# Attention with a spline feed-forward layer: chunk 2 staged ahead of the first feed-forward tile, and three moves ahead of it

## The chip, the cores and the metric

One of the cores of a Trainium2 chip runs the whole kernel. The metric is the device time of one execution in microseconds (us), as the median of several. The engines are named as in the profile: PE (TensorE, matmuls and transposes), PEld (its weight loads), DVE (VectorE), ACT (ScalarE), POOL (GpSimd) and SP (SyncE, which here only issues DMAs; ACT has a DMA queue of its own, ACTq).

## The reference

x has shape (4, 512, 512). Cut to what matters:

```python
xn = layernorm(x)                                  # last axis
q, k, v = xn @ Wq + bq, xn @ Wk + bk, xn @ Wv + bv # 16 heads of 32
scores = q k^T / sqrt(32) + slope(head) * distance(key), causal
attn = softmax(scores) v ;  a = attn @ Wo + bo
gate_w, up_w = spline(gate_cp), spline(up_cp)      # (2048, 512), Catmull-Rom
down_w = spline(down_cp)                           # (512, 2048)
f = (silu(xn @ gate_w.T) * (xn @ up_w.T)) @ down_w.T
out = x + a + f
```

The dense weights of the feed-forward layer are interpolated from about 8,100 control points each: every weight is a blend of four neighbouring points with cubic coefficients.

## The kernel before

The kernel has two parts that every engine runs one after the other: `attention` for all four batches, then `ffn`. Both keep fp32 accuracy by splitting operands into a rounded high part and a remainder ("hi" and "lo") and multiplying in three terms. Each engine's order is written out by hand; semaphores connect the engines, and an engine that waits holds up all that stands behind it in its list. SP issues its DMAs in list order too.

Attention. A batch has H = 16 steps, one per head, and each step has four query tiles. In step s, PE makes the scores of head s (line 689), DVE adds the distance bias and takes the maximum (`bias_and_max`, line 910), ACT takes the exponentials and casts them (lines 1143, 1151), POOL makes their low part (line 1256), PE turns the probabilities of step s-2 (line 703) and weighs the values of step s-3 (lines 720, 723). DVE and ACT copy the turned tiles (lines 919, 1158), DVE normalizes (928 to 936). `UNITS`, `TURNS` and `SPLITS` say in which step a projection, a transposition or a split of the values stands; the next batch's layer norm and projections are carried along in steps 7 to 15 of the running batch. Scores take queries and keys from stacks that SP copies there after POOL's low part (line 1311). `v_split` (lines 889 to 900) makes three bf16 parts of the values of one token tile in three DVE instructions, behind a first cast on ACT (`v_high`, line 1136). In the first batch the values of tiles 0 to 3 are taken ahead of step 0, tiles 0 and 1 are split at the end of step 0 together with tile 2, and tile 3 in step 1 (`FIRST_SPLITS`).

Layer norm of a later batch: DVE makes mean and variance (`pair_stats`), POOL the inverse deviation (line 1244), DVE the shift -mean * rstd (`norm_shift`, line 869), and ACT applies both in one activation per tile (line 1103) in steps 8 and 9.

Weights of the feed-forward layer. They come in five chunks: chunk 0 for down, chunks 1 to 4 for gate and up, four tiles of 128 rows in each. A chunk is a load of blend factors (1 MB) and one of control windows ("taps", 1 MB), seven DVE instructions that blend them (`taps_op`, lines 343 and 348, 0 to 6), a split into high (ACT, `taps_high`, line 358) and low (DVE, `taps_low`, line 368) for the two halves m = 0, 1 of the partitions, and DMAs that copy each half across to the other 64 partitions (`copy_across`, lines 376 and 380, four of 128 KB for chunks 1 to 4). The input of gate and up is the tile z: windows of the turned input (line 330) and moments of it over pieces (line 335), loaded per tile and per quarter of four tiles. Moments are products of bases with the turned input; the last batch's are made in the attention part, the others in `ffn` (kind "mom").

`ffn` runs the batches in the order 3, 0, 1, 2, with 16 tiles of the hidden dimension each. `ffn_order` writes PE's order: for each tile k "gu" (four matmuls, lines 1588 and 1589), in the first batch a "gen" (four matmuls, lines 1576 and 1577) that makes one tile of the down weights, and "down" of tile k-2 (twelve matmuls, lines 1601 to 1603). A generated tile goes through ACT (`down_start`, 1642), DVE (`merge`, 1706), ACT (`down_high`, 1656) and DVE (`down_low`, 1710). Two gens stand ahead of tile 0; `GEN_FRONT` and `GEN_BACK` place the others. `TAPS` places the blending of chunks 2 (its low split only), 3 and 4 on DVE, `HIGHS` their high split on ACT, and ACT issues the copies a tile later. In the first batch gate and up always use the same pair of banks.

At the seam SP's list is: the moments of the last batch, bases for gen, windows of tiles 0 to 3, moments, bases, the turned input of the next batch (two loads of 1 MB), factor 3, windows of tiles 4 to 7, moments, three attention sums (line 1328), taps 3 and 4, the fourth sum; then, once all sums are stored (line 1824), factor 4, bases, windows of tiles 8 to 15 and moments. DVE's list there: the last low context (943), the output sums (950) with the blending of chunk 2 and the low split of chunk 1 between them.

## Time and profile before

| | |
|---|---|
| median of 3 runs | 746.64 us (746.29 to 746.75) |
| the profiled execution | 748.68 us, span 746.9 us, mean granted clock 0.975 |
| PE busy | 673.0 us (90%) |
| PEld, DVE, ACT, POOL busy | 540.0, 463.3, 451.8, 322.3 us |
| DMA traffic | 110.15 MB, mean 147 GB/s |
| chain that ended last | PE 42%, POOL 5%, DVE 4%, issue 4%, ACT 2%, DMA 2% of the span |

Sizes of the transfers at the seam, from the page's list of DMA issues: factor and taps 1024 KB each, a load of turned input 1024 KB, bases for gen 512 KB, a window load 88 KB (two per tile), a moment load 160 KB, a copy across 128 KB, an attention sum 256 KB.

Busy shares are means over the whole span; matmuls overlap, and a busy PE is not one at its peak. The granted clock is the share of 2.4 GHz that PE was allowed in a stretch. A row of a timeline has its start and length in us; what stands in brackets at its end is the time for which the engine had been idle and what released it ("issue": nothing that the profile shows as an engine's work, often a DMA).

### The profile page before, as it was taken

The page shows a single profiled execution, that of the slowest core. Times are in us where ns is not written, and L with a number is a line of the kernel's source. Part 1 is how long each engine was busy: PE and PEld are TensorE (multiplying, and loading weights), DVE is VectorE, ACT ScalarE, POOL GpSimd, SP SyncE. Part 2 cuts the span into 40 slices and gives each one's busy share as a digit, 9 for nine tenths or more (in the row PEclk, how much of TensorE's full clock was granted, in tenths as well). Part 3 has the DMA queues.
Part 4 walks back from the last instruction along what each step waited for, and adds up shares of the span by engine and source line. Part 5 has one row for each costly group of instructions (what it writes and reads, how often), then busy time and mean ns, then how long its engine had stood idle before and what let it go on. Part 6 is the DMA issues. An engine that isn't in the chain of part 4 may idle for free.

```text
span 746.9 us, 13707 instructions
## 1 busy us (share of the span) xinstructions
PE 673.0 (90%) x4884; PEld 540.0 (72%) x4884; DVE 463.3 (62%) x1287; ACT 451.8 (60%) x717; POOL 322.3 (43%) x188
## 2 busy tenths in 40 slices
PE   4977889989799898899898876888999999999997
PEld 3756678777577776777776665666888888888885
DVE  6477977879877879778799796567441223223212
ACT  5478887877977878878779763444442332332221
POOL 0255554544644545545546430222253236236334
PEclk9988999999999999999999999899999999999999
DMA  9749497476676384863947939874576484244001
GB/s 304 115 71 225 86 259 128 64 135 169 94 204 86 43 140 98 216 86 57 208 76 97 400 97 271 255 220 113 163 245 213 130 244 166 70 143 140 13 1 56
DMA packets 53355, 110.15 MB, mean 147 GB/s; under 512 B 6504, under 2 KB 6760, under 8 KB 51752
## 3 DMA queue, kind: packets, MB, share of 16 engines
q1 hardware_dynamic: 51704, 106.85, 58.6%
q10 hardware_dynamic: 1584, 2.43, 1.3%
q8 instruction: 39, 0.64, 0.4%
q14 instruction: 28, 0.23, 0.1%
HBM read 59.32 MB, written 25.17 MB: 113 GB/s over the span
## 4 chain that ended last, share of the span: by engine, by line
PE 42%; POOL 5%; DVE 4%; issue 4%; ACT 2%; DMA 2%; ACTq 0%; SPq 0%; POOLq 0%; DVEq 0%
PE bank L1601 6%; PE bank L1603 6%; PE bank L1602 6%; PE bank L1588 3%; PE bank L1589 3%; POOL resid L1769 3%; PE bank L615 3%; PE bank L703 3%; PE bank L617 2%; PE bank L616 2%; DMA taps<-windows 2%; PE bank L689 2%; POOL in_lo L1761 1%; PE bank L1576 1%; PE bank L720 1%
## 5 line engine op out<-in xcount | busy, mean ns | idle before, releaser
L1256 POOL TENSOR_TENSOR work<-work 128x1280 f16<-128x1280 f32 x64 | 170.9, 2670 | 174.2 <-ACT work L1151 174.2
L1761 POOL TENSOR_TENSOR in_lo<-inner,in_hi 128x512 fp32r<-128x512 f32 x64 | 83.0, 1299 | 200.0 <-ACT in_hi L1668 200.0
L910 DVE CUSTOM_DVE_ANT_0 work<-bank,dist 128x128 f32<-128x128 f32 (+3 forms) x256 | 115.3, 487 | 59.4 <-PE bank L689 44.9
L1143 ACT ACTIVATE work<-work,neg_max 128x128 f32<-128x128 f32 (+3 forms) x256 | 129.3, 562 | 18.2 <-DVE neg_max L910 18.1
L1718 DVE TENSOR_TENSOR inner<-bank,silu 128x512 f32<-128x512 f32 x64 | 44.1, 688 | 132.3 <-ACT silu L1662 130.7
L1668 ACT CAST in_hi<-inner 128x512 fp32r<-128x512 f32 x64 | 39.7, 620 | 135.2 <-PE bank L1603 134.4
L703 PE MATMUL bank<-ident,work 128*128 128x128 f16 x1280 | 106.0, 226 | 14.6 <-DVE work L919 10.3
L703 PEld LDWEIGHTS bank<-ident,work 128*128 128x128 f16 x1280 | 75.4, 101 | 51.3 <-issue 31.8
L1151 ACT CAST work<-work 128x1280 f16<-128x1280 f32 x64 | 80.6, 1259 | 49.8 <-PE bank L703 48.6
L1601 PE MATMUL bank<-w_room,in_hi 128*128 128x512 f32 x256 | 100.0, 391 | 0.7 <-POOL in_lo L1761 0.7
L1602 PE MATMUL bank<-w_room,in_hi 128*128 128x512 f32 x256 | 99.6, 389 | 0.0
L1603 PE MATMUL bank<-w_room,in_lo 128*128 128x512 f32 x256 | 99.6, 389 | 0.0
L689 PE MATMUL bank<-k_stack,q_stack 96*128 96x256 f32 (+2 forms) x256 | 76.2, 373 | 22.4 <-DVE neg_max L910 18.3
L919 DVE COPY work<-bank 128x256 f16<-128x256 f16 (+2 forms) x192 | 75.6, 418 | 5.8 <-PE bank L703 5.7
L689 PEld LDWEIGHTS bank<-k_stack,q_stack 96*128 96x128 f32 x256 | 45.5, 195 | 38.7 <-DVE neg_max L910 29.6
L720 PE MATMUL bank<-v_parts,work 128*128 128x98 bf16 x640 | 66.7, 211 | 2.0 <-issue 2.0
L1158 ACT COPY work<-bank 128x1024 f16<-128x1024 f16 x64 | 64.4, 1006 | 2.5 <-PE bank L703 2.5
L723 PE MATMUL bank<-v_parts,work 128*128 128x66 bf16 x640 | 64.1, 195 | 0.0
L1588 PE MATMUL bank<-z,wgu_hi 128*128 128x512 f32 x128 | 52.2, 408 | 11.6 <-issue 7.5
L1601 PEld LDWEIGHTS bank<-w_room,in_hi 128*128 128x128 f32 x256 | 48.4, 189 | 12.0 <-POOL in_lo L1761 2.0
L720 PEld LDWEIGHTS bank<-v_parts,work 128*128 128x128 f16 x640 | 52.7, 99 | 5.6 <-issue 2.8
L1602 PEld LDWEIGHTS bank<-w_room,in_hi 128*128 128x128 f32 x256 | 48.1, 188 | 9.9
(113 smaller groups left out, 1313.9 us busy)
## 6 DMA issues: line engine op xcount, KB each, us to landing
q_stack<-parts SPq DMA_DIRECT2D x48, 256.0 KB, 5.8
k_stack<-parts SPq DMA_DIRECT2D x48, 256.0 KB, 6.2
z<-xt_scratch SPq DMA_DIRECT2D x128, 88.0 KB
x_in<-x SPq DMA_DIRECT2D x32, 256.0 KB, 6.7
xt_scratch<-xt_room SPq DMA_DIRECT2D x8, 1024.0 KB, 7.5
xt_room<-xt_scratch SPq DMA_DIRECT2D x6, 1024.0 KB, 10.6
factor<-c_basis SPq DMA_DIRECT2D x5, 1024.0 KB, 11.8
taps<-windows SPq DMA_DIRECT2D x5, 1024.0 KB, 15.8
```

The costliest lines, as they stand in the source:

```text
L689: pe.matmul(score_bank[i % 2][:, 0:n], q_stack[:, at, h, i * P:(i + 1) * P], k_stack[:, at, h, 0:n], start=True, stop=True).then_inc(s_ful ...
L703: mm = pe.transpose(pt_bank[i % 2][:, (part * n + k) * P:(part * n + k + 1) * P], probs16[:, s % 2, part, OFF[i] + k * P:OFF[i] + (k + 1) ...
L720: pe.matmul(bank[:, i * VALUES:(i + 1) * VALUES], probs_t[:, s % 2, at:at + P], v_parts[:, k, s, :], start=(k == 0), stop=False)
L910: dve.tensor_tensor_reduce(probs[:, s % 2, OFF[i]:OFF[i] + n], score_bank[i % 2][:, 0:n], dist[:, S - n:S], -slope(s), 3.4e38, ALU.add, AL ...
L919: dve.tensor_copy(probs_t[:, s % 2, 2 * OFF[i]:2 * OFF[i] + n], pt_bank[i % 2][:, 0:n]).then_inc(pt_free[i % 2], 1)
L1143: e = act.activation(tile, tile, ACT.Exp, bias=neg_max[:, s % 2, i:i + 1], scale=-1.0)
L1151: act.copy(probs16[:, s % 2, 0, :], probs[:, s % 2, :]).then_inc(hi_ready, 1)
L1256: pool.tensor_tensor(probs16[:, s % 2, 1, :], probs[:, s % 2, :], probs16[:, s % 2, 0, :], ALU.subtract).then_inc(lo_ready, 1)
L1601: pe.matmul(sum_bank[i][:, :], hi, wd_hi[:, g, :], start=(g == 0), stop=False)
L1602: pe.matmul(sum_bank[i][:, :], hi, wd_lo[:, g, :], start=False, stop=False)
L1603: mm = pe.matmul(sum_bank[i][:, :], lo, wd_hi[:, g, :], start=False, stop=(g == NG - 1))
L1761: pool.tensor_tensor(in_lo[k % 2][:, :], inner[:, k % 2, :], in_hi[:, k % 2, :].bitcast(F32), ALU.subtract).then_inc(il_ready, 1)
```

## The change

- The value splits of tiles 0 to 2 of the first batch stand between the takings of the values, ahead of step 0, and that of tile 3 in step 0. ACT's four first casts all stand ahead of step 0.
- For later batches DVE makes only -mean (with the statistics), and ACT multiplies it with the inverse deviation, one [128 x 1] activation per tile, ahead of its norm_apply.
- The first blending instruction of chunk 1 moves from step 12 to step 13 of the last batch.
- `taps_low` and `copy_across` wait for their own half m only. Of chunk 1's high casts on ACT one moves behind the last context cast; on DVE its low splits stand around `ctx_low`.
- All copies across of chunks 1 to 4 are issued by SP, no longer by ACT: chunk 1's behind the first moments, chunk 2's behind the moments of quarter 1, chunk 3's behind the windows of tiles 8 to 15, chunk 4's between the moment stores.
- SP loads the turned input of the next batch right after the moments' stores; taps 3 stands among the windows of tiles 4 to 7, taps 4 behind all four sums.
- Only one gen stands ahead of tile 0, the others one tile later; gen 10 stands behind tile 10's gate and up. Chunk 2 is split high and low around gen 0's first steps, ahead of tile 0.

```diff
+        def taps_high(act, c, some=(0, 1)):
-            eng.wait_ge(made_hi[c], 2)
+            eng.wait_ge(made_hi[c], m + 1)          # taps_low
-            eng.wait_ge(made_lo[c], 2)
+                eng.wait_ge(made_lo[c], m + 1)      # copy_across, per m
...
-FIRST_SPLITS = {0: [(0, 2)], 1: [(0, 3)]}
+FIRST_SPLITS = {0: [(0, 3)]}
...
+            if later(b):
+                dve.tensor_scalar(minus_mean[:, two], meanvar[:, two, 0], -1.0, None, ALU.mult).then_inc(mean_ready, 1)
...
-            if carry and s in (8, 9):
-                norm_shift(b + 1, s - 8)
-            if not later(b) and s == 0:
-                v_split(b, 0, 0)
-                v_split(b, 0, 1)
...
             v_take(0, t)
+            if t < 3:
+                v_split(0, 0, t)
...
-            if s >= H - 4:
+            if s == H - 3:
+                taps_op(dve, 1, 0)
+            if s >= H - 3:
                 taps_op(dve, 1, s - H + 4)
...
+        taps_low(dve, 1, 0)
         ctx_low(B - 1, KC - 1)
+        taps_low(dve, 1, 1)
...
+        def norm_shift(b, n):                       # on ACT
+            act.wait_ge(mean_ready, 2 * (b - 1) + n + 1)
+            act.wait_ge(rstd_ready, 2 * b + n + 1)
+            for t in (2 * n, 2 * n + 1):
+                act.activation(shift[:, t:t + 1], minus_mean[:, t:t + 1], ACT.Copy, scale=rstd[:, t:t + 1]
+                               ).then_inc(shift_ready, 1)
...
-        for t in range(3):
+        for t in range(QT):
             v_high(0, 0, t)
...
-                taps_high(act, 1)
+                taps_high(act, 1, (0,))
         ctx_high(B - 1, KC - 1)
+        taps_high(act, 1, (1,))
         act.activation(warm[:], ident[0:1, 0:1], ACT.Silu)
-        copy_across(act, 1)
...
+        sp.wait_ge(xt_st, 32 * B)
+        load_turned(sp, 1)
         sp.wait_ge(lo_ready, H * B)
...
         load_moments(sp, 0, 0)
+        copy_across(sp, 1)
         load_pieces(sp, 1)
-        load_turned(sp, 1)
         load_factor(sp, 3)
         sp.wait_ge(av_full, H * B)
-        for g in range(4, 8):
+        for g in range(4, 6):
+            load_windows(sp, 0, g)
+        sp.wait_ge(pj_full, pj_total(("o", QT - 1), B - 1))
+        load_taps(sp, 3)
+        for g in range(6, 8):
             load_windows(sp, 0, g)
         load_moments(sp, 0, 1)
-        for q in range(QT - 1):
+        copy_across(sp, 2)
+        for q in range(QT):
             store_sum(B - 1, q)
-        sp.wait_ge(pj_full, pj_total(("o", QT - 1), B - 1))
-        load_taps(sp, 3)
         load_taps(sp, 4)
-        store_sum(B - 1, QT - 1)
...
-GEN_FRONT = {k: k + 2 for k in range(MOM_STEPS[0] + 1)}
-GEN_BACK = {k: k + 1 for k in range(MOM_STEPS[1] + 1, NG - 1)}
+GEN_FRONT = {k: k + 1 for k in range(MOM_STEPS[0] + 1)} | {MOM_STEPS[1] + 1: MOM_STEPS[1] + 1}
+GEN_BACK = {-1: 0} | {k: k + 1 for k in range(MOM_STEPS[1] + 1, NG - 1)}
-    order = [("gen", 0, 0, 1), ("gen", 1, 0, 1)]
+    order = [("gen", GEN_BACK[-1], 0, 1)]
-TAPS = {1: [(2, 7)], 2: [(3, 0), (3, 1)], 3: [(3, 2), (3, 3)], 4: [(3, 4), (3, 5), (3, 6)], 5: [(3, 7), (4, 0)],
-        6: [(4, 1), (4, 2)], 7: [(4, 3), (4, 4)], 8: [(4, 5), (4, 6)], 9: [(4, 7)]}
-HIGHS = {0: 2, 4: 3, 8: 4}
+TAPS = {2: [(3, 0), (3, 1)], 3: [(3, 2), (3, 3), (3, 4)], 4: [(3, 5), (3, 6)],
+        5: [(3, 7), (3, 8), (4, 0)], 6: [(4, 1), (4, 2)], 7: [(4, 3), (4, 4)], 8: [(4, 5), (4, 6)], 9: [(4, 7), (4, 8)]}
+HIGHS = {4: 3, 8: 4}
...
-        for g in range(2):                          # ffn_scalar
-            down_start(g)
-            down_high(g)
+        taps_high(act, 2, (0,))
+        down_start(0)
+        taps_high(act, 2, (1,))
-                if n - 1 in HIGHS:
-                    copy_across(act, HIGHS[n - 1])
...
-        for g in range(2):                          # ffn_vector
-            merge(g)
-            down_low(g)
+        taps_low(dve, 2, 0)
+        merge(0)
+        taps_low(dve, 2, 1)
...
-        for g in range(8, 12):                      # ffn_sync
-            load_windows(0, g)
-        load_moments(0, 2)
+        for q in (2, 3):
+            for g in range(4 * q, 4 * q + 4):
+                load_windows(0, g)
+            load_moments(0, q)
+        copy_across(sp, 3)
         sp.dma_start(bm[:].bitcast(F32).rearrange("p k e n -> p (k e n)"), moment_d).then_inc(bm_ld, 16)
-        for g in range(12, NG):
-            load_windows(0, g)
-        load_moments(0, 3)
         load_pieces(3)
-        for m in range(3):
-            store_moment(1, m)
+        store_moment(1, 0)
+        store_moment(1, 1)
+        copy_across(sp, 4)
+        store_moment(1, 2)
```

## Rows read from the trace of the kernel before

**Rows 1.** Windows: stretch, length, busy (xcount) of PE PEld DVE ACT POOL, clock
```profile
100.00:140.00 40.00, 39.77 (x360) 31.80 (x361) 29.14 (x98) 31.50 (x48) 19.67 (x9) 1.00 0.78 184
```

**Rows 2.** Timeline, prologue: start, length, engine, line, operation, [idle before <-releaser]
```profile
38.55 2.88 DVE L896 TENSOR_TENSOR v_room<-v_room,v_parts 128x256 f32<-128x256 f32 x1
...
43.28 0.29 DVE L910 CUSTOM_DVE_ANT_0 work<-bank,dist 128x128 f32<-128x128 f32 x1
...
60.30 0.29 DVE L910 CUSTOM_DVE_ANT_0 work<-bank,dist 128x128 f32<-128x128 f32 x1 [3.77 <-issue]
...
24.36 4.76 POOL L1277 TENSOR_TENSOR w_room<-work,w_room 128x1024 fp32r<-128x1024 f32 x2 [14.79 <-ACT w_room L1199]
...
38.51 2.63 POOL L1256 TENSOR_TENSOR work<-work 128x1280 f16<-128x1280 f32 x1 [9.39 <-ACT work L1151]
...
38.83 0.47 PE L689 MATMUL bank<-k_stack,q_stack 96*128 96x256 f32 x2 [2.15 <-issue]
```

**Rows 3.** The shift's line; the timeline of ACT; the groups of ACT
```profile
L869 DVE SCALAR_TENSOR_TENSOR shift<-meanvar,rstd x6: 554/956/1353, 85.3 to 297.9; 128x2 f32<-128x2 f32 x6
...
93.57 1.52 ACT L1103 ACTIVATE x_in<-x_in,shift,rstd 128x512 f32<-128x512 f32 x2 [0.55 <-DVE shift L869]
...
L1143 ACT ACTIVATE work<-work,neg_max 128x128 f32<-128x128 f32 x64 | 26.2, 410 | 8.1 <-DVE neg_max L910 8.1
...
L1237 ACT ACTIVATE warm<-ident 1x1 f32<-1x1 f32 x1 | 0.2, 202 | 0.0
```

**Rows 4.** Timeline of DVE and of PE, last batch, step 12
```profile
419.65 1.37 DVE L343 TENSOR_TENSOR taps<-taps,factor 128x512 f32<-128x512 f32 x1 [2.44 <-DMA taps<-windows]
...
417.94 0.40 PE L689 MATMUL bank<-k_stack,q_stack 96*128 96x256 f32 x2
```

**Rows 5.** Timeline of DVE, then of PE, where they waited
```profile
450.17 0.69 DVE L943 TENSOR_TENSOR ctx_t<-bank,ctx_t 128x512 fp32r<-128x512 f32 x1 [1.99 <-ACT ctx_t L1164]
...
464.33 0.77 PE L1588 MATMUL bank<-z,wgu_hi 128*128 128x512 f32 x1 [2.33 <-issue]
...
487.16 0.76 PE L1588 MATMUL bank<-z,wgu_hi 128*128 128x512 f32 x1 [2.95 <-issue]
...
504.40 0.50 PE L1588 MATMUL bank<-z,wgu_hi 128*128 128x512 f32 x1 [1.77 <-DVE inner L1718]
...
511.50 0.47 PE L1588 MATMUL bank<-z,wgu_hi 128*128 128x512 f32 x1 [2.27 <-issue]
```

**Rows 6.** The windows view of PE alone, before and after tile 8
```profile
464.33:511.50 47.17, 37.90 (x137) 0.87 0.82 239
...
511.50:549.00 37.50, 37.50 (x164) 1.00 0.48 139
```

**Rows 7.** Timeline of the DMA issues, on SP's and ACT's queue
```profile
450.85 0.82 SPq L335 DMA_DIRECT2D z<-moment_scratch  x2
...
452.11 0.97 SPq L314 DMA_DIRECT2D xt_room<-xt_scratch  x2
...
461.40 4.60 SPq L1328 DMA_DIRECT2D mid_scratch<-x_in  x3
...
466.06 1.10 SPq L305 DMA_DIRECT2D taps<-windows  x2
...
487.34 0.33 SPq L1825 DMA_DIRECT2D factor<-c_basis  x1
...
503.58 0.94 SPq L335 DMA_DIRECT2D z<-moment_scratch  x2
...
455.76 0.78 ACTq L380 DMA_DIRECT2D wgu_lo<-wgu_lo  x1
```

**Rows 8.** Landing of the copies, then the DMA view's issues
```profile
DMA to landing us min/median/max: 4.7/7.0/7.9
...
mid_scratch<-x_in SPq DMA_DIRECT2D x4, 256.0 KB, 15.3
```

**Rows 9.** Windows of SP: stretch, length, granted clock, DMA share, GB/s
```profile
444.00:448.00 4.00, 1.00 0.33 94
```

More of the change, by code:

```diff
@@ L351, in tiles_of @@
             return room[m * ZR:(m + 1) * ZR, m, 4 * (c - 1):4 * c, :].rearrange("p g n -> p (g n)")
-        def taps_high(act, c):
+        def taps_high(act, c, some=(0, 1)):
             act.wait_ge(made[c], 7)
-            for m in range(2):
+            for m in some:
                 rows = slice(m * ZR, (m + 1) * ZR)
@@ L560, in attention @@
     shift = sb("shift", [P, QT], F32)
+    minus_mean = sb("minus_mean", [P, QT], F32)
     minus_half = sb("minus_half", [P, QT], F32)
@@ L582, in attention @@
     (ident_ld, const_ld, dist_ld, wh_ready, wl_ready, wl_pool, small_set,
-     pj_full, ln_stats, ln_mv, ln_var, rstd_ready, shift_ready, xn_ready, xh_ready,
+     pj_full, ln_stats, ln_mv, ln_var, rstd_ready, mean_ready, shift_ready, xn_ready, xh_ready,
      full_ready, ql_ready, v_rest, v_mid, vh_ready, v_done, s_full, t_done, p_ready, hi_ready,
@@ L586, in attention @@
         ctx, "ident_ld", "const_ld", "dist_ld", "wh_ready", "wl_ready", "wl_pool", "small_set", "pj_full", "ln_stats", "ln_mv",
-        "ln_var", "rstd_ready", "shift_ready", "xn_ready", "xh_ready", "full_ready", "ql_ready", "v_rest", "v_mid",
+        "ln_var", "rstd_ready", "mean_ready", "shift_ready", "xn_ready", "xh_ready", "full_ready", "ql_ready", "v_rest", "v_mid",
         "vh_ready", "v_done", "s_full", "t_done", "p_ready", "p_hi_ready", "p_lo_ready",
@@ L864, in norm_apply @@
                               ALU.subtract, ALU.mult).then_inc(xn_ready, 1)
-        def norm_shift(b, n):
-            two = slice(2 * n, 2 * n + 2)
-            dve.wait_ge(rstd_ready, 2 * b + n + 1)
-            dve.scalar_tensor_tensor(shift[:, two], meanvar[:, two, 0], -1.0, rstd[:, two], ALU.mult, ALU.mult
-                                     ).then_inc(shift_ready, 1)
         def x_low(b, t):
@@ L1077, in attention_vector @@
                     taps_low(dve, 0, m)
+        taps_low(dve, 1, 0)
         ctx_low(B - 1, KC - 1)
+        taps_low(dve, 1, 1)
         taps_op(dve, 2, 0)
         add_residual(B - 1, 0)
-        for m in range(2):
-            taps_low(dve, 1, m)
         add_residual(B - 1, 1)
@@ L1098, in x_high @@
                      pj_bank[bank][:, :].rearrange("p (c n) -> p c n", c=KC)).then_inc(xh_ready, 1)
+        def norm_shift(b, n):
[4 more added lines that the diff above has]
+                               ).then_inc(shift_ready, 1)
         def norm_apply(b, t):
-            if t % 2 == 0:
-                act.wait_ge(shift_ready, 2 * (b - 1) + t // 2 + 1)
+            act.wait_ge(shift_ready, QT * (b - 1) + t + 1)
             act.activation(x_in[:, t, :], x_in[:, t, :], ACT.Identity, bias=shift[:, t:t + 1],
@@ L1170, in step @@
                 if carry and s in (8, 9):
+                    norm_shift(b + 1, s - 8)
                     norm_apply(b + 1, 2 * (s - 8))
@@ L1415, in attention_sync @@
         sp.wait_ge(pt_full, QT * H * B)
-        sp.wait_ge(xt_st, 32 * B)
         sp.wait_ge(pad_st, 16)
@@ L1668, in inner_high @@
             act.copy(in_hi[:, k % 2, :], inner[:, k % 2, :]).then_inc(ih_ready, 1)
-        for g in range(2):
-            down_start(g)
-            down_high(g)
-        for kind, n, half, _ in ORDER[2:]:
+        taps_high(act, 2, (0,))
+        down_start(0)
+        taps_high(act, 2, (1,))
+        for kind, n, half, _ in ORDER[1:]:
             if kind == "gu":
@@ L1726, in add_down @@
                                   ).then_inc(sum_ready, 1)
-        for g in range(2):
-            merge(g)
-            down_low(g)
-        for kind, n, half, _ in ORDER[2:]:
+        taps_low(dve, 2, 0)
+        merge(0)
+        taps_low(dve, 2, 1)
+        for kind, n, half, _ in ORDER[1:]:
             if kind == "gu":
@@ L1741, in ffn_vector @@
                     else:
-                        taps_low(dve, c, 0)
-                        taps_low(dve, c, 1)
+                        taps_low(dve, c, i - 7)
                     if at == 0 and n in GEN_FRONT:
```

## The prediction, before the changed kernel was run

> **What bounds the kernel now.** The page first: TensorE (PE) is busy most of the span, so only stretches where PE stands still or runs slowly can pay. The windows view says where it doesn't pay to look: in 100:140 PE is busy 39.77 of 40 us [rows 1]. A time gained ahead of such a stretch is kept, since what follows waits on engines and on transfers that engines release, all of which move with it. The timelines then give four places.
>
> Prologue: the second attention step's scores stand at 38.83, but DVE takes them at 43.28, because it sits in the third value split, whose subtraction lasts 2.88 us beside POOL's 38.51 instruction [rows 2]. At step 4 DVE waits 3.77 us for the stacked keys of chunk 1 [rows 2]; these leave only after step 1's casts, so they come earlier by what step 1 gains.
>
> Steps 8 and 9 of each carried batch: the shift on DVE, six times, 0.554 to 1.353 us, and ACT once waits 0.55 us for it [rows 3].
>
> Step 12 of the last batch: DVE stands 2.44 us for the control windows of chunk 1, and the first product then takes 1.37 us [rows 4].
>
> First feed-forward batch: gate and up of tile 0 start at 464.33 after 2.33 us of a wait that no engine ends, tile 4 after 2.95, tile 7 after 1.77 for DVE, tile 8 at 511.50 after 2.27 [rows 5]; tile 2 is a second case of the tile 7 kind (2.28 us at 473.27). From tile 0 to tile 8 PE takes 47.17 us for 137 matmuls at a granted clock of 0.87; after it, 164 take 37.50 us at 1.00, which is 0.2287 us each [rows 6]. So 47.17 stands against 31.1 (136 × 0.2287): 16 us of excess, the largest pool in the kernel.
>
> **Part 1, value splits.** The third split leaves the space between steps 0 and 1. Upper bound of the gain: 43.28 less about 39.2, when the scores are in the bank, 4.1 us. Against it: the splits now stand between the value sums, beside POOL's pair of weight subtractions (24.36, 4.76 us) [rows 2]. If the first split's two contended instructions wait for those two, it ends near 29.7 instead of 27.3, the later sums follow, and step 0 starts near 34.9 instead of 33.6; ACT's exponentials then carry some of that into step 1, and less what it saves by one cast it no longer does in step 0. I take 3.3 us (bounds 0 and 4.1), near the upper row because DVE is free before 38.83 in either case.
>
> The Trainium skill ("GPSIMD Engine Reference", Specifications) says that GpSimd shares its SBUF interfaces with VectorE and collides with instructions of two SBUF inputs. The subtraction of 2.88 us has two, and agrees with it. By that rule the new place is partly as bad as the old one; without it the term would be 4.1.
>
> **Part 2, the shift.** DVE loses 0.55 and 1.35 us per batch and gains two tiny scalings of about 0.1 to 0.17 us, so about 1.6 us less. But ACT gets four [128 x 1] activations per batch and a wait on its own result ahead of norm_apply; queued behind it are the cast of the probabilities, its share of the turned tiles and PE's transposes. A 1x1 activation takes 0.202 us, the 128x128 one 410 ns [rows 3]. ACT runs without a gap through steps 8 and 9 apart from the 0.55 us wait for the shift, which goes. With 0.4 us per pair: 2 × 0.4 - 0.55 = 0.25 us later per batch, 0.7 us lost over three. Bounds: DVE decides instead (3 × 1.2 = 3.6 us gained), or each costs 0.41 (12 × 0.41 = 4.9 lost). I take 0.7 lost, since ACT's row is the one without slack.
>
> **Part 3, chunk 1 blended from step 13.** The 2.44 us wait and the 0.6 us of work leave step 12. PE starts the next scores at 417.94 [rows 4]; DVE could take them at 418.3 instead of 421.0 (419.65 + 1.37): 2.6 us gained. The windows land at 419.6 and are then wanted near 422.6, and the moved 0.6 us falls in step 13, after which DVE idled 1.48 us, so it costs nothing. Without that cover it costs 0.6. Bounds 1.5 and 3.
>
> **Part 4, entry of the first feed-forward batch.** ACT's last context cast now has one cast of chunk 1 before it, not two, so DVE's 1.99 us wait [rows 5] shrinks by 0.6 and the output projection ends that much earlier. The copies of chunk 1 to the other half were issued on ACT's queue until 455.76 + 0.78 = 456.5 [rows 7]; with a landing of 7 us and more [rows 8] that gives 464.3, the start of tile 0. Now SP issues them right behind the moments of quarter 0, over at 451.7 (450.85 + 0.82 [rows 7]): four issues of about 0.6 end at 454.1. The reloading of the turned input, 2 MB, formerly ahead of factor 3 from 452.11 [rows 7], goes to 440, where the DMA engines are at a share of 0.33 [rows 9], and factor 3 is behind the copies. Landing then by 457 to 460. PE is done with the one generated tile near 458.6, DVE with the last sum near 459.0; I take 459.3 for tile 0, 5.0 us earlier. Chunk 2 is split around tile 0's merge, some 1.3 us each on ACT and DVE, where PE has gate and up to do.
>
> **Part 5, tile 0 to tile 8.** ACT's issuing of four copies between two tiles, about 3 us at 0.78 each [rows 7], goes (it made tile 7's 1.77), and so does tile 4's wait: copy 2 leaves SP about 465, tile 4 is due about 476. What is late next is SP. It issues everything in order, and behind "all sums stored" stand factor 4, the windows of tiles 8 to 15, the moments and only then the copies of chunk 3. Sums now leave at 467.5 with one load of windows (taps 3) ahead of them; before, both (466.06) were ahead of the last, and SP went on at 487.34 [rows 7]. From 452 on, by the sizes given with the profile, the queue has to move 0.5 (copies) + 0.5 (bases) + 1 (factor 3) + 0.7 (eight window loads) + 0.3 (moments) + 1 (taps 3) + 0.5 (copies) + 1 (sums) = 5.5 MB until the last sum is stored; at 239 GB/s [rows 6] that is 23 us, so 475. The series from 487.34 to 503.58 + 0.94 [rows 7], less 0.35 for a load that moves behind, is 16.8 us: 491.8. Copies issued to 494.2, landed near 497 (about 3 us, the queue being light; ten of theirs in the row would say 501). Tile 8 thus starts at 497, 37.7 us after tile 0 instead of 47.17: 9.5 us earlier. Given back: by tile 8 one generated tile fewer has been made, 4 × 0.2287 = 0.9 us. Bounds for parts 4 and 5: 3.6 (copies land as late as the sums, 15.3 us [rows 8]) and 19 (nothing waits, 31.1 us plus about 2 to start). Value 5.0 + 9.5 - 0.9 = 13.6.
>
> **Sum.** 3.3 - 0.7 + 2.6 + 13.6 = 18.8 us. The profiled execution took 748.68 (span 746.9), so 729.9 in such an execution; that one run lies 2.04 above the median 746.64 of the three, so 727.8.
>
> **Rivals.**
> A, backlog on SP's queue. The copies share the ring with windows and taps: they land 7 us later than I said, tile 8 at 504, time 734.8. For it: the sums took 15.3 us on that queue while ACT's copies took 7.0 [rows 8]. Against: 2 MB went ahead and one load of windows goes behind.
> The Trainium skill ("DMA: Bandwidth & Descriptors", Queues, rings and completion order) says that each DMA engine alternates between the queue rows and takes one row's descriptors in order. That speaks against giving up ACT's own row, and it names this rival.
>
> B, PE is the bound throughout: stores land by 470, tile 8 at 492, the clock stays at 1.00 and the prologue gives 4.1. 727.8 - 5 - 0.8 = 722.
>
> C, the tiny activations cost as the 128x128 one does: 4.9 instead of 0.7 lost, 732.
>
> D, slower: copies land as taps and sums do, 16 to 17 us after their issue. Copy 3 issued till 494.2 lands 511, moment stores follow, copy 4 is issued near 524.5 and lands at 541, where tile 12 started at about 534: 7 us later than before. With 5.9 gained by parts 1 and 3 and 0.7 lost, 748.5. It decides from a landing of about 15 us for copy 4; against it, the DMA engines were nearly empty there.
>
> **How the numbers follow.** Forecast 0.58 (its own range 724 to 731.5), A 0.20, B 0.13, C 0.06, D 0.03. The range 720.5 to 737 leaves out D, the far end of A and of B. A difference under 0.2% (1.5 us) counts as none. Faster 0.95, same 0.02, slower 0.03.
>
> **What would show it.** In the new trace: step 1's first score taken by DVE near 39.5 and step 4's near 57; no DVE wait at step 12; tile 0's gate some 10 us after DVE's last context subtraction (before: 464.33 - 450.17 = 14.2); no wait at tiles 4 and 7; one at tile 8 that a DMA ends; granted clock above 0.90 from tile 0 to 8. I am wrong if PE waits at tile 0 or 4 for a copy, or if tile 8 to 16 takes over 40 us.

## The result, and the profile after

After the change the kernel takes 740.23 us (median of 5 runs, 737.79 to 740.77), before it 746.29 (5 runs, 744.31 to 746.75): ratio 0.9917, 95% interval 0.9895 to 0.9938, so 0.8% less. Forecast were 727.8 and a range from 720.5 to 737. The profiled executions, 739.71 against 748.68, lie 9.0 us apart and the medians 6.1, since before's profiled one is 2.4 above its median and after's 0.5 below. The steps are followed in the profiled pair; of its 9.0 us about 3 are not in the medians.

The table has the start of VectorE's (DVE) first bias instruction of an attention step and of the first gate matmul of a feed-forward tile, in us. Attention steps are counted from 0 through all batches (step 61 is step 13 of the last), tiles from 0 through all batches too.

| place | before | after | gained |
|---|---|---|---|
| step 1 | 43.28 | 38.77 | 4.5 |
| step 3 | 52.14 | 46.92 | 5.2 |
| step 4 | 60.30 | 57.68 | 2.6 |
| step 16 | 135.57 | 133.44 | 2.1 |
| step 48 | 341.86 | 338.70 | 3.2 |
| step 61 | 420.94 | 414.95 | 6.0 |
| step 63 | 433.05 | 428.61 | 4.4 |
| tile 0 | 464.33 | 457.24 | 7.1 |
| tile 4 | 487.16 | 474.95 | 12.2 |
| tile 8 | 511.50 | 499.76 | 11.7 |
| tile 9 | 520.24 | 509.88 | 10.4 |
| tile 11 | 529.37 | 520.46 | 8.9 |
| tile 63 | 732.69 | 723.73 | 9.0 |

How far one pair of executions can be trusted, the profiles of the experiments below show. Eight of them (those on chunk 3's copies, the basis, the windows, the turned input, chunk 1's copies and the blending) have the code of the change up to step 48. In seven, step 16 starts between 132.60 and 134.01 and step 48 between 337.88 and 339.30; the eighth, the slowest run of the blending in steps 13 and 14, is at 136.22 and 342.10. From step 16 to 48 the eight take 205.27 to 206.50 us.

In the head and the chain of the page of after, PE stands where it stood; what is new in the chain is time of SyncE's queue (SPq) and of the copies into the gate-up tiles:

```profile
PE 665.9 (90%) x4884; PEld 535.3 (73%) x4884; DVE 458.3 (62%) x1287; ACT 452.7 (61%) x729; POOL 322.6 (44%) x188
...
PE 42%; POOL 4%; issue 4%; DVE 3%; SPq 3%; DMA 2%; ACT 1%; POOLq 0%; DVEq 0%; ACTq 0%
```

The windows view of after for 100 to 140 us (PE full, as in [rows 1]), and of PE alone from tile 0 to tile 8 and for as long behind it as in [rows 6] (length, busy, clock, DMA share, GB/s):

```profile
100.00:140.00 40.00, 40.00 (x369) 32.01 (x368) 29.65 (x98) 30.48 (x48) 18.79 (x9) 1.00 0.72 171
...
457.24:499.76 42.52, 33.39 (x137) 0.92 0.81 232
499.76:537.26 37.50, 37.00 (x156) 0.96 0.53 161
```

Tile 0 to 8 takes 42.5 us instead of 47.2 [rows 6]; 37.7 were forecast. The waits of after that answer to those of [rows 5], in PE's timeline:

```profile
457.24 0.47 PE L1594 MATMUL bank<-z,wgu_hi 128*128 128x512 f32 x1 [2.38 <-DMA wgu_lo<-wgu_lo]
...
463.89 0.50 PE L1594 MATMUL bank<-z,wgu_hi 128*128 128x512 f32 x1 [1.04 <-DVE inner L1722]
...
474.95 0.47 PE L1594 MATMUL bank<-z,wgu_hi 128*128 128x512 f32 x1 [1.70 <-DMA wgu_lo<-wgu_lo]
...
499.76 0.77 PE L1594 MATMUL bank<-z,wgu_hi 128*128 128x512 f32 x1 [6.39 <-issue]
...
515.75 0.50 PE L1582 MATMUL bank<-coef,bd 128*128 128x512 f32 x1 [0.50 <-DVE mom_st L1701]
```

Tile 7's wait is gone. Tiles 0 and 4 now wait for a copy by name. Tile 8 waits nearly three times as long as before (6.39 us, then 2.27), and its first matmul then takes 0.77 us, not 0.47. The windows of PE show the clock beside it. In the wait nothing runs; behind it the granted clock is 0.50, the lower level (1.2 GHz), and later 0.95:

```profile
493.40:499.70 6.30, 0.00 (x0) 0.70 0.85 215
499.76:501.80 2.04, 2.04 (x5) 0.50 0.99 406
502.00:510.00 8.00, 8.00 (x35) 0.95 0.04 17
```

The wait is marked "issue"; SPq's timeline shows what it was:

```profile
435.36 1.20 SPq L314 DMA_DIRECT2D xt_room<-xt_scratch  x2
...
458.93 0.53 SPq L380 DMA_DIRECT2D wgu_hi<-wgu_hi  x1
...
461.49 3.37 SPq L1331 DMA_DIRECT2D mid_scratch<-x_in  x4
464.90 0.50 SPq L305 DMA_DIRECT2D taps<-windows  x1
477.41 0.33 SPq L1828 DMA_DIRECT2D factor<-c_basis  x1
...
478.26 7.33 SPq L330 DMA_DIRECT2D z<-xt_scratch  x8
...
486.55 6.46 SPq L330 DMA_DIRECT2D z<-xt_scratch  x8
...
495.84 1.03 SPq L380 DMA_DIRECT2D wgu_lo<-wgu_lo  x1
```

The last copy of chunk 3 is issued at 495.84, and the landing times of that chunk's copies (the view of tile wgu_lo, 490 to 500 us) are

```profile
DMA to landing us min/median/max: 3.7/3.8/3.8
```

so it is there at 499.6, and tile 8 starts at 499.76. Between its issues at 464.90 and 477.41 SyncE stood for the stores of the sums, 11.9 us in all:

```profile
SPq L1827 <- DMA mid_scratch<-x_in: 11.9, 2, 11.3
```

### The profile page after: what moved, and what is told of

The parts are those of the page before. It is cut to its first block, busy times and chain, and to the rows that moved or that the text cites. A ratio compares the mean times of both kernels' runs of the same rounds, so it can differ in the third digit from the quotient of the medians.

```text
span 737.9 us, 13725 instructions
## 1 busy us (share of the span) xinstructions
PE 665.9 (90%) x4884; PEld 535.3 (73%) x4884; DVE 458.3 (62%) x1287; ACT 452.7 (61%) x729; POOL 322.6 (44%) x188
## 4 chain that ended last, share of the span: by engine, by line
PE 42%; POOL 4%; issue 4%; DVE 3%; SPq 3%; DMA 2%; ACT 1%; POOLq 0%; DVEq 0%; ACTq 0%
PE bank L1607 7%; PE bank L1609 6%; PE bank L1608 6%; PE bank L704 3%; PE bank L1594 3%; PE bank L1595 3%; POOL resid L1772 3%; PE bank L616 2%; PE bank L690 2%; DMA wgu_lo<-wgu_lo 2%; PE bank L618 2%; PE bank L617 2%; SPq L330 2%; POOL in_lo L1764 1%; PE bank L721 1%
## 5 line engine op out<-in xcount | busy, mean ns | idle before, releaser
L1153 ACT CAST work<-work 128x1280 f16<-128x1280 f32 x64 | 80.6, 1259 | 47.9 <-PE bank L704 47.2
L1594 PE MATMUL bank<-z,wgu_hi 128*128 128x512 f32 x128 | 51.2, 400 | 11.5 <-issue 6.4
L1607 PEld LDWEIGHTS bank<-w_room,in_hi 128*128 128x128 f32 x256 | 48.0, 188 | 11.9 <-POOL in_lo L1764 1.9
L1609 PEld LDWEIGHTS bank<-w_room,in_lo 128*128 128x128 f32 x256 | 48.0, 188 | 10.0
```

The costliest lines, as they stand in the source:

```text
L1153: act.copy(probs16[:, s % 2, 0, :], probs[:, s % 2, :]).then_inc(hi_ready, 1)
L1607: pe.matmul(sum_bank[i][:, :], hi, wd_hi[:, g, :], start=(g == 0), stop=False)
L1609: mm = pe.matmul(sum_bank[i][:, :], lo, wd_hi[:, g, :], start=False, stop=(g == NG - 1))
```

## The experiments

All are the change with one edit, unless they say otherwise; ratios are to the kernel before, with 95% intervals. The interval of the change itself, 0.9895 to 0.9938, is what each is held against. The kernel before, run again beside them, had medians from 746.14 to 747.50, so a difference in us from the change's 740.23 is good to about 1 us. Where one is compared with the change at a place, both are profiled executions.

### Chunk 3's copies earlier

```diff
         for q in (2, 3):
             ...
             load_moments(0, q)
+            if q == 2:
+                copy_across(sp, 3)
-        copy_across(sp, 3)
```

> The changed kernel with the four copies of chunk 3 issued by SP ahead of the windows of tiles 12 to 15 instead of behind them. Theory (SP's list order is what tile 8 waits for: copies issued at 493.98 to 496.87 in the changed kernel): the copies leave SP near 487 to 490, land by 494, PE's 6.39 us wait at tile 8 shrinks to under 1 us, and 5 to 7 us are gained over the changed kernel (about 0.984 of the kernel before). Rival (the DMA engines are full, not SP's list): the wait at tile 8 stays above 4 us and the time within 1.5 us of the changed kernel.

Measured: 737.79 us (737.37 to 739.36), ratio 0.9874 (0.9849 to 0.9899). In PE's timeline tile 8 starts without a wait, 6.6 us earlier, and the next one is new, for the basis `bm`, which SyncE still issues behind the last windows, at 496.47:

```profile
493.19 0.39 PE L1594 MATMUL bank<-z,wgu_hi 128*128 128x512 f32 x1
...
503.00 0.60 PE L1570 MATMUL bank<-xt_room,bm 128*128 128x512 f32 x1 [5.11 <-issue]
```

So the copies' place in SyncE's order was what tile 8 waited for, as the theory had it. One load behind them takes most of it back: tile 9 is 1.1 us earlier, and the interval of the ratio touches the change's.

### Chunk 3's copies and the basis load earlier

```diff
+            if q == 2:
+                copy_across(sp, 3)
+                sp.dma_start(bm[:]..., moment_d).then_inc(bm_ld, 16)
-        copy_across(sp, 3)
-        sp.dma_start(bm[:]..., moment_d).then_inc(bm_ld, 16)
```

> The copies of chunk 3 and the load of the moment bases both ahead of the windows of tiles 12 to 15. In the first experiment tile 8 started 6.6 us earlier, but PE then waited 5.11 us for the bases (issued 496.5) ahead of the moments, and only 1.1 us were left at tile 9. Theory (SP's list order holds both): bases issued near 489, landed by 495, no wait at the moments, tile 9 near 503 to 504, 5 to 6 us gained over the changed kernel. Rival (the DMA engines have no room there): the bases land after 500 all the same, or tile 12 waits for its windows, and under 2 us are gained.

Measured: 731.58 us (730.46 to 733.06), ratio 0.9806 (0.9783 to 0.9829), 8.65 us below the change. PE from tile 0 to 8, and behind:

```profile
457.50:492.26 34.76, 32.10 (x136) 1.00 0.89 266
492.26:529.76 37.50, 36.26 (x160) 1.00 0.62 176
```

The last copy is issued at 487.13, 8.7 us earlier, the clock stays at 1.00, and tile 9 stands at 500.92 instead of 509.88. Nothing but SyncE's order differs, so the wait at tile 8 and the slow clock behind it cost 8 to 9 us. That is more than the 5 to 6 us of the theory, which had no price for the clock.

### Windows ahead of the wait for the sums

```diff
+        for g in range(8, 12):
+            load_windows(0, g)
+        load_moments(0, 2)
         for q in range(QT):
             sp.wait_ge(res_st[q], 16 * B)
         sp.dma_start(factor[4][:], c_factor[4])...
         load_pieces(2)
-        for q in (2, 3):
-            for g in range(4 * q, 4 * q + 4):
-                load_windows(0, g)
-            load_moments(0, q)
+        for g in range(12, NG):
+            load_windows(0, g)
+        load_moments(0, 3)
```

> The changed kernel with the windows and moments of tiles 8 to 11 issued ahead of the wait for the stored sums, in which SP otherwise stands 11.9 us. Theory (tile 8 waits for SP's list, whose pace is set by the landing of the sums): SP goes on after the sums with 7 us less to do, the copies of chunk 3 leave by 487 to 490, the wait at tile 8 goes, 5 to 7 us gained over the changed kernel. Rival (full DMA engines): the window loads stand ahead of nothing but delay taps 4 and the sums, the sums are stored 3 us later, and under 3 us are gained.

Measured: 743.35 us (738.53 to 747.52), ratio 0.9943 (0.9918 to 0.9969). No gain, so the theory was wrong. The queue's wait was not idle time to be filled: the DMA engines were busy in it (in the change a share of 0.99 from 464 to 472). The windows took their place among the loads, and factor 4, issued at 479.23, took 16.5 us to land (4.9 in the change). It came late for DVE, which works in order:

```profile
495.79 0.69 DVE L343 TENSOR_TENSOR taps<-taps,factor 128x512 f32<-128x512 f32 x1 [6.69 <-DMA factor<-c_basis]
```

Tile 7 then waited 4.94 us for DVE and tile 8 another 3.58. This profiled execution is the slowest of its twelve (747.52), so its waits may be on the long side.

### The turned input loaded late

```diff
-        sp.wait_ge(xt_st, 32 * B)
-        load_turned(sp, 1)
         sp.wait_ge(lo_ready, H * B)
         ...
+        sp.wait_ge(xt_st, 32 * B)
         ...
         load_taps(sp, 4)
+        load_turned(sp, 1)
```

> The changed kernel with the 2 MB of turned input issued behind taps 4 instead of ahead of the first windows. Theory (from 436 to 477 the DMA engines are full, so that 2 MB ahead of everything push back the copies of chunks 1 and 2, whose landing tiles 0 and 4 wait for, and the sums): the waits at tiles 0 and 4 (2.38, 1.70 us) go, SP goes on after the sums 5 to 8 us earlier, near 470, tile 8 and tile 9 start 5 to 8 us earlier. Rival (the move used slack, as I predicted): the waits grow or stay and the time is the changed kernel's or worse.

Measured: 738.98 us (736.62 to 744.66), ratio 0.9912 (0.9877 to 0.9947), no difference from the change. The first half of the theory came, the second did not. Tile 0 starts at 455.30, tile 4 at 471.30 without a wait, and factor 4 is issued at 472.84 instead of 477.41. The engines were indeed backed up by the 2 MB: the low copies (wgu_lo) now land 3.6 to 4.4 us after their issue for chunk 1 (6.2 to 8.0 in the change) and 7.3 to 7.8 for chunk 2 (12.5 to 14.1), the sums 7.8 to 8.9 (12.9 to 14.0). But tile 8 has gained nothing: of chunk 3's four copies three land 3.5 to 4.3 us after their issue and the last, issued at 491.30, 8.5 us after it. The 2 MB are issued ahead of them now, but had landed by about 481, so that they slow the last copy is not shown; why it took that long stays open.

```profile
499.88 0.77 PE L1594 MATMUL bank<-z,wgu_hi 128*128 128x512 f32 x1 [8.72 <-DMA wgu_lo<-wgu_lo]
```

### Both: copies and basis early, turned input late

> The change with chunk 3's copies and the basis load ahead of windows 12 to 15, and the loads of the turned input behind the fourth taps. The first edit alone gave 731.6, the second alone 739.0. Theory: the 16 DMA engines are full from 440 to 472 us, and what counts is the bytes ahead of each copy; the turned loads are not needed before tile 9, so behind the taps they free 5 us for copies 1 and 2 (tile 0 at 455.3, tile 4 without a wait), and chunk 3's copies, issued at about 481, are ahead of everything that is left: 728 to 730 us. Rival: in the second edit alone the copies of chunk 3 landed 8 us after their issue because the turned loads stood just ahead of them; with both edits they still do, tile 8 waits 2 to 6 us for a DMA, and the time is 732 to 736.

Measured: 736.84 us (735.47 to 737.07), ratio 0.9872 (0.9847 to 0.9897), 5.3 above the version with copies and basis early alone. The theory was wrong, and its rival right in the wait at tile 8, which is even longer: chunk 3's copies are issued till 484.6, the low ones take 10.5 to 12.6 us to land, and tile 8 waits for them. The turned loads had landed by about 480.5, just ahead of the first copy's issue (480.94), so they act through what they held up: factor 4, issued at 472.04, takes 10.3 us to land (4.9 in the change).

```profile
DMA to landing us min/median/max: 10.5/11.6/12.6
...
496.77 0.77 PE L1594 MATMUL bank<-z,wgu_hi 128*128 128x512 f32 x1 [6.84 <-DMA wgu_lo<-wgu_lo]
```

### Chunk 1's copies on ScalarE's queue

```diff
         act.activation(warm[:], ident[0:1, 0:1], ACT.Silu)
+        copy_across(act, 1)
-        copy_across(sp, 1)
```

> The changed kernel with the four copies of chunk 1 on ACT's queue again, issued behind its table load. Theory (in SP's ring they stand behind 2 MB of turned input and the windows; a ring of its own is served beside it): last copy landed by 454, tile 0 starts near 455 without a wait, and SP issues the rest 2.8 us sooner; 2 us gained. Rival (it is the DMA engines and not the ring order that are full): landing as late as in the changed kernel (7 us after issue), tile 0 at 457 or later, no gain.

Measured: 740.19 us (738.1 to 740.81), ratio 0.9915 (0.9892 to 0.9937), the change's own. Issued at much the same time (446.2 to 449.4), they landed no sooner, and tile 0 waits 2.87 us: the rival was right. Landing of the wgu_lo copies of chunk 1, here and then in the change:

```profile
DMA to landing us min/median/max: 6.3/8.2/10.1
```
```profile
DMA to landing us min/median/max: 6.2/7.1/8.0
```

The Trainium skill ("DMA: Bandwidth & Descriptors", Queues, rings and completion order) says that each DMA engine takes turns between the queue rows it has work for. By that a copy on ACT's row should pass what waits on SyncE's; these landings don't show it.

### The old place of the splits, the shift, the blending

Three runs, each undoing one part. The splits again behind step 0:

```diff
-            if t < 3:
-                v_split(0, 0, t)
+            if not later(b) and s == 0:
+                v_split(b, 0, 0)
+                v_split(b, 0, 1)
```

> The changed kernel with the value splits of the first batch at their old places. Theory (the splits' move gains 5 us up to step 3 and loses half of it again at step 4, where the stacked keys of chunk 1 land later after their issue): step 4's first score is taken 2.6 us later than in the changed kernel and the whole is 2 to 3 us slower. Rival (the gain at step 3 is lost altogether later): no difference within 0.5 us at step 16. Second rival (my prediction's 3.3): 3 us or more.

Measured: 742.53 us (741.88 to 743.0), ratio 0.9934 (0.991 to 0.9958): 2.3 us by the medians, as the theory had it, but by the ratios the two overlap. Step 4 is at 59.63 instead of 57.68, step 16 at 135.77, later than in any version with the new place at its usual speed (132.60 to 134.01). At tile 4 only 0.6 us are left and at the end 2.2.

The shift again on DVE:

```diff
-            act.activation(shift[:, t:t + 1], minus_mean[:, t:t + 1], ACT.Copy, scale=rstd[:, t:t + 1])
+            dve.scalar_tensor_tensor(shift[:, two], meanvar[:, two, 0], -1.0, rstd[:, two], ALU.mult, ALU.mult)
```

> The changed kernel with the shift made by DVE again, in one instruction per pair. Theory (DVE sets the pace in steps 8 to 10, so the move gained about 1 us in three batches: by the step starts 0.0, 0.2 and 0.8): step 48 starts 0.7 to 1.3 us later than in the changed kernel, the whole is 1 us slower. Rival (the prediction: ACT sets the pace and the two tiny activations cost 0.25 us per batch): 0.7 us faster than the changed kernel.

Measured: 741.1 us (738.25 to 743.33), ratio 0.9914 (0.9884 to 0.9945): by the time no difference. In the trace step 48 is 0.70 later and steps 16 to 48 take 205.74 us, not 205.26. Both lie inside what eight executions without this edit show (up to 339.30, and 205.27 to 206.50), so neither a gain nor a loss is shown. ACT's new instructions cost 0.284 us each, where I had taken 0.2:

```profile
L1100 ACT ACTIVATE shift<-minus_mean,rstd x12: 277/284/296, 84.2 to 296.5; 128x1 f32<-128x1 f32 x12
```

The blending of chunk 1 again from step 12:

```diff
-            if s == H - 3:
-                taps_op(dve, 1, 0)
-            if s >= H - 3:
+            if s >= H - 4:
```

> The changed kernel with the first blending of chunk 1 back in step 12. Theory (2.6 us gained at step 13, 1.2 of them lost at step 14, because the second of the two instructions now runs into POOL's and takes 3.10 us): step 13 starts 2.3 to 2.8 us later than in the changed kernel, step 15 1.0 to 1.5 us later, the whole 1 to 1.5 us slower. Rival (my prediction, all of it kept): 2.6 us slower. Second rival (the seam is full of DMAs and takes everything back): no difference at tile 0.

Measured: 741.61 us (738.4 to 743.66), ratio 0.9931 (0.9903 to 0.9958), which overlaps the change's. DVE waits again for the windows:

```profile
415.70 1.67 DVE L343 TENSOR_TENSOR taps<-taps,factor 128x512 f32<-128x512 f32 x1 [2.13 <-DMA taps<-windows]
```

From step 60 to 63 it takes 21.41 us instead of 19.39, where every other version of the change takes 18.99 to 19.65: the move is worth about 2 us there.

### The blending in steps 13 and 14

```diff
             if s == H - 3:
                 taps_op(dve, 1, 0)
-            if s >= H - 3:
+            if s == H - 2:
+                taps_op(dve, 1, 1)
+            if s >= H - 2:
```

> The change with the three blending operations of chunk 1 placed anew: the first in step 13 as in the change, the other two in step 14, none in step 15. Theory: 1.2 of the 2.6 us that were expected of the blending are given back because the second operation, at 420.1 us, meets GpSimd's low half (2.88 us beside 3.10) just ahead of VectorE's maxima; in step 14 it meets that step's low half instead, and step 15's maxima come sooner: the last step's start goes from 428.61 to about 427.5, and the time falls by about 1. Rival: any place between two steps costs the same, because each step of VectorE beside GpSimd is full; two operations in one step then delay step 15 by 1 to 2 us more than the change does, and the time rises by 0 to 1.5.

A fourth product stays in step 15, which the expectation had wrong. Measured: 740.56 us (736.59 to 746.28, 12 runs), ratio 0.9927 (0.9902 to 0.9951), no difference. Its profiled execution is its slowest, so only distances are read: step 60 to 63 takes 19.61 us, in the change 19.39. The collision is really there in the change (first DVE's timeline, then POOL's), and it moved along with the instructions (the last line, of the edit, beside a POOL instruction of 429.32):

```profile
419.53 3.70 DVE L343 TENSOR_TENSOR taps<-taps,factor 128x512 f32<-128x512 f32 x2
...
419.80 2.88 POOL L1259 TENSOR_TENSOR work<-work 128x1280 f16<-128x1280 f32 x1 [2.71 <-ACT work L1153]
```
```profile
429.05 3.69 DVE L343 TENSOR_TENSOR taps<-taps,factor 128x512 f32<-128x512 f32 x2
```

Alone a blending instruction takes 0.68 us. Two steps without one between them start sooner, and the next gives it back: the rival was right.

### The high copies of a stack first

```diff
+                early = not later(b) and c in (1, 2)
+                if early:
+                    bank, used = pj_use(("qk"[m], c), b)
+                    sp.wait_ge(pj_free[bank], used + 1)
-                sp.wait_ge(ql_ready, 8 * b + 2 * c + m + 1)
+                else:
+                    sp.wait_ge(ql_ready, 8 * b + 2 * c + m + 1)
                 ...
+                    if early and low:
+                        sp.wait_ge(ql_ready, 8 * b + 2 * c + m + 1)
```

> The change with one edit: for chunks 1 and 2 of batch 0 SyncE issues the two copies of a stack that take the high part as soon as that part is written, and the third, of the low part, when GpSimd has written it. Theory: of the 4.5 to 5.2 us won by step 3 the half is lost before step 4 because the six stack copies are the bound there: from 44 to 54 us the DMA engines are busy to 1.09 of the span at 128 GB/s, and q's and k's copies (1.5 MB together, 12 us at that rate) now stand back to back, where they had a gap of 3 us before the change. If so, q's copies start 2.5 us earlier (40.2 instead of 42.7), and step 4 begins 1.5 to 2.5 us earlier than 57.68, between 55.2 and 56.2. Rival 1: it is the latency of one k copy after its issue (8.1 us) that counts: the last copy still waits for GpSimd's low part at 47.7, step 4 moves by under 0.5. Rival 2: step 4 moves, but what is won is given back as in the change itself, under 0.3 us are left at the end.

Measured: 736.25 us (734.04 to 737.81), ratio 0.9861 (0.9834 to 0.9887). Windows of SyncE in the prologue (length, clock, DMA share, GB/s), first before, then the change:

```profile
43.00:49.00 6.00, 0.68 0.92 131
49.00:52.00 3.00, 1.00 0.03 3
52.00:58.00 6.00, 1.00 0.92 128
```
```profile
44.00:50.00 6.00, 1.00 1.10 146
50.00:56.00 6.00, 0.97 1.06 128
```

Before, q's three copies and k's three have a pause between them; after, they fill the DMA engines without one, at 146 and then 128 GB/s. With the high copies first (SPq, then DVE):

```profile
39.95 3.17 SPq L1323 DMA_DIRECT2D q_stack<-parts  x3
44.80 3.35 SPq L1323 DMA_DIRECT2D k_stack<-parts  x3
...
54.72 0.29 DVE L907 CUSTOM_DVE_ANT_0 work<-bank,dist 128x128 f32<-128x128 f32 x1 [3.54 <-issue]
```

Step 4 comes 2.96 us earlier, more than the theory's 1.5 to 2.5, and 2.65 are there at step 63. By the first rival step 4 would have moved by under 0.5, so it is the start of the six copies that held it. At tile 4 1.93 are left (its wait for chunk 2's copies is 4.14 now) and at the end 1.92. A part of an earlier attention is waited off behind the full DMA engines. By the medians 4.0 us are gained; the profiled execution is the slowest of its six.

### Three edits together

Copies and basis early, high copies first, blending in steps 13 and 14.

> The change with chunk 3's copies and the basis load ahead of windows 12 to 15 (731.6 alone), the high copies first in batch 0, and the blending in steps 13 and 14. If the three act in places of their own, the gains add: 731.6 less what the other two give alone beside it. If an earlier start of the feed-forward is only waited off behind the full DMA engines, the sum is 1 to 2 us short of that.

Measured: **728.71 us** (727.85 to 729.08), ratio 0.9764 (0.9737 to 0.9792), the fastest version, 17.5 us below the kernel before and 11.5 below the change. Tile 8 starts at 489.89 without a wait; of the waits for copies only tile 4's is left, 1.47 us:

```profile
471.65 0.47 PE L1605 MATMUL bank<-z,wgu_hi 128*128 128x512 f32 x1 [1.47 <-DMA wgu_lo<-wgu_lo]
```

Over the copies and basis alone (731.58) it brings 2.9; the high copies alone brought 4.0 by the medians and 1.9 by the profiles, the blending nothing. The interval of the ratio overlaps that of copies and basis alone (0.9783 to 0.9829), and the runs of the high copies spread over 3.8 us, so the runs don't tell whether 1 us is lost in the adding.

## Why the prediction was wrong

The whole was faster, as forecast, and the time was won in the places named. But of the 18.8 us forecast 6.1 are in the medians and 9.0 in the profiled pair. By terms, in the profiled pair:

| part | forecast | measured |
|---|---|---|
| splits | +3.3 | +2.1 (step 16) |
| shift | -0.7 | +1.0 (step 16 to 48; inside the spread, see below) |
| chunk 1 | +2.6 | +1.3 (step 48 to 63; 1.0 from step 60 to 63, 2.0 there when undone alone) |
| tile 0 | +5.0 | +2.7 |
| tile 0 to 8 | +9.5 | +4.6 |
| tile 8 to 11 | -0.9 | -2.8 |
| sum | 18.8 | 9.0 |

**The step that failed is "at 239 GB/s [rows 6] that is 23 us, so 475"**, the time at which SyncE gets past the stored sums. The 475 is in before's time; after's is 4.44 us less, what was gained by step 63. SyncE got past the stored sums at 477.41 + 4.44 = 481.9, 6.9 us late, and tile 8 came at 499.76 + 4.44 = 504.2, 7.2 late. Everything behind that wait went as worked out: the series to the moments took 16.5 us (forecast 16.8), the copies landed 3.8 us after their issue (3). So the 475 was wrong and what followed it right. Windows of SyncE in after (share, GB/s last):

```profile
440.00:448.00 8.00, 1.00 0.98 308
448.00:456.00 8.00, 1.00 1.04 202
456.00:464.00 8.00, 0.79 1.03 282
464.00:472.00 8.00, 1.00 0.99 245
472.00:476.00 4.00, 1.00 0.71 241
```

From 448 to 476 the engines moved (202 + 282 + 245) x 8 + 241 x 4 = 6.8 MB, 243 GB/s in the mean. The rate of 239 was right; I had counted 5.5 MB. What was missing in the count can be estimated from sizes and issue times:

- My 5.5 are in units of 1024 KB, which is 5.8 MB in the unit of this view.
- The queue was not empty when my count began. From 435.36, when the turned input was issued, to 448 some 4.3 MB were issued, and 274 x 4 + 308 x 8, so 3.6 MB, were moved from 436 on (274 GB/s is the rate from 436 to 440). Of the rest 0.3 are the first two copies, which I had counted; about 0.5 MB is backlog.
- That leaves 0.5 MB, which is of taps 4. It is issued right behind the sums, at 464.90, and lands 14.9 us later, at 479.8, so it moves partly beside them. I had not counted it.

The backlog is the turned input's. Its two loads took 6.2 and 8.6 us to land, till 444.6, and the windows behind them came that much later. I had read the share of 0.33 [rows 9] as room for 2 MB. In before the shares from 440 to 452 are 0.55, 0.33 and 0.55, so 6.3 us of the 12 were free; 2 MB at 365 GB/s, after's rate from 440 to 444, fill 5.7 of them, and next to nothing is left. The experiments are the stronger proof: loading it late brought factor 4's issue forward by 4.6 us, and by 4.5 where copies and basis are early (472.04 instead of 476.55). That is two thirds of the 6.9; the other 2.3 us no run took apart. The Trainium skill ("DMA: Bandwidth & Descriptors", Queues, rings and completion order) says that one row's descriptors are taken in order. The runs agree: what was put ahead (windows, the turned input) came out as later landings behind.

**Tile 0.** It waited 2.38 us for chunk 1's copies, which were issued till 449.6 and landed 8 us later (457.0); forecast was "by 457 to 460" in before's time, which is 453 to 456. It is the same backlog: with the turned input late, tile 0 starts at 455.30. That was one of the two signs that I had named for being wrong; the other (tile 8 to 16 over 40 us) came too, 42.5 us (499.76 to 542.22).

**Behind tile 8** my 0.9 for one generated tile was right: tile 10 to 11 is 1.45 us longer, 0.9 and the wait of 0.50 for DVE. What I left out is the clock: after 6.39 us of standing, tile 8 to 9 takes 10.12 us instead of 8.74. With the copies early it is 8.66. A long wait is dearer than its length.

**Rival A** had the mechanism and the number for tile 8 (504) and a chance of 0.20. Its time, 734.8, was still 5.4 low: 0.8 for parts 1 to 3, 2.1 for the rest (mostly what is lost behind tile 8), and 2.6 for the profiled executions (I took 2.04 above the median, and after's lies 0.52 below its own). My reasons against it, 2 MB ahead and one load behind, were wrong on the first half.

**Splits.** Step 1's score was taken at 38.77 (forecast about 39.5) and step 4's at 57.68 (near 57). 4.5 to 5.2 us were won, more than my 3.3 and, in the first steps, more than my bound of 4.1. I had said that the stacked keys of chunk 1 "come earlier by what step 1 gains". They didn't: the six stack copies had a pause of 3 us to lose, and then they were the bound. Their issue went forward by 4.0 us (51.73 to 47.71) and step 4 by 2.6. The run with the high copies first bears it out: with them issued sooner, step 4 comes 2.96 us earlier. The first split did meet POOL's pair (its cast of 26.57 took 2.37 us), and step 0 was taken at 34.50 instead of 33.64, where I had said 34.9.

**Shift.** My loss of 0.7 us isn't shown, and no gain is either: steps 16 to 48 take 206.29 us before and 205.26 after, and eight other executions with the new shift take 205.27 to 206.50. What the move costs ACT or saves DVE stays open, within about 1 us. Rival C, 4.9 lost, is out: the activations cost 0.284 us, not 0.41, and none of these executions takes over 0.2 us more there than before. (My other bound had a slip: 1.6 us a batch make 4.8, not 3.6.)

**Chunk 1.** DVE took the scores of step 13 (61 in the table) without standing for the windows, 5.73 us after those of step 12 instead of 8.32: the forecast 2.6. In the next step 1.2 us went back (8.21 us instead of 7.01), where the second instruction met POOL's, and 0.3 in the one after. I had priced the moved 0.6 us at nothing for the idle of 1.48 us behind it. But the moved instruction pushed the one behind it into POOL's, and together they take 3.70.

Rival B's picture (tile 8 without a wait, clock 1.00) is what the version with copies and basis early reaches, with tile 8 near 496 in before's time, not at 492, and 731.58 us in all, not 722. Rival D did not happen: chunk 4's copies, issued at 512.66, held nobody up at tile 12.

## What to carry to other kernels

Before a transfer is moved ahead because "the DMA engines are nearly idle there", write down the bytes issued from that point in order, with the time at which each is wanted, and start the sum where the engines next become full, not where the change's own loads start. Count what is issued right behind the last one too. What stands behind a completion wait on an in-order queue pays for all bytes ahead of the wait: order such a queue by when things are wanted, as the copies and the basis here, wanted at tiles 8 and 9, ahead of windows wanted at tiles 12 to 15. And where a gain makes two groups of copies touch that had a pause between them, it ends at the sum of their times.

## What the runs showed of the hardware

The copies into the stacks, 256 KB each from one SBUF tile to 32 partitions of another, fill the DMA engines at a low rate: a share of 1.06 at 128 GB/s, while 308 GB/s stand at 0.98 where loads from DRAM run. The Trainium skill ("DMA: Bandwidth & Descriptors", Where 436 GB/s comes from) has the fabric, 435 GB/s, as the bound between SBUF and SBUF; this trace gives about a third of it or less for these copies (128 to 146 GB/s). Why was not tried.

Two DVE instructions of 0.68 us took 3.70 together beside one of POOL (2.88), the same in another step (3.69). The loss behind a long wait was the third thing I had not put a price on. Ten versions (the change and nine experiments) have a wait of 3.58 to 8.72 us ahead of tile 8, and in them tile 8 to 9 takes 10.12 to 11.60 us. In before, with a wait of 2.27, it takes 8.74, and in the two versions without a wait and with the basis early 8.66 and 8.64, at a granted clock of 1.00. So such a wait costs 1.4 to 3.0 us beyond itself, and not by its length alone: 8.72 us cost 2.7, 5.60 cost 2.9.
